# A two-block recurrent/attention kernel: one small weight product from rounded parts and residues, and the second row group's normalisation ahead of three chunks

## The reference, cut to what matters

```
xn = layernorm(x)
s  = attn(xn)                      # layer 0: recurrent cell, layer 1: attention
g  = silu(ffn(xn, W1, W2, W3))     # silu(xn W1^T) * (xn W3^T), Hadamard transform, times W2^T
x  = x + s * g
```

```
out = ((xn @ W_in^T) * k) @ W_out^T      # = xn @ M,  M = W_in^T diag(k) W_out^T, 256 x 256
s   = xn + rmsnorm(out) * norm_w
```

## Time and profile before

| what | value |
|---|---|
| time, median of 3 runs | 355.51 us (355.45 to 355.77) |
| the profiled execution | 356.1 us, of which the span of the trace is 354.3 us |
| PE busy | 348.0 us, 98% of the span |
| DVE busy | 250.6 us, 71% |
| ACT busy | 170.4 us, 48% |
| POOL busy | 108.3 us, 31% |
| granted TensorE clock | full (1.00) through the whole span |

### The profile page before, as it was taken

One profiled execution on the slowest core, in us unless ns is written; L12 is line 12 of the kernel. 1 busy time (PEld: TensorE's weight loads), 2 busy tenths in 40 slices (PEclk: granted clock), 3 DMA queues, 4 the chain that ended last, 5 costly groups with the idle time before them and its releaser, 6 DMA issues.

```text
span 354.3 us, 4946 instructions
## 1 busy us (share of the span) xinstructions
PE 348.0 (98%) x1761; PEld 295.3 (83%) x1761; DVE 250.6 (71%) x491; ACT 170.4 (48%) x336; POOL 108.3 (31%) x125
## 2 busy tenths in 40 slices
PE   7999999999999999999999999999999999999996
PEld 4877888888888888888978878888888888888896
DVE  5679964995589766967588886787657887367624
ACT  2855452447245613445365544654446444464531
POOL 2163510365226943664015030160300703004011
PEclk9999999999999999999999999999999999999999
DMA  8989759306161403140242501526014251064001
GB/s 259 221 185 225 150 105 120 100 2 159 20 159 20 120 0 118 27 125 0 89 146 49 136 0 59 170 50 194 8 42 153 74 152 57 0 192 127 9 0 61
DMA packets 69664, 34.44 MB, mean 97 GB/s; under 512 B 40708, under 2 KB 69640, under 8 KB 69640
## 3 DMA queue, kind: packets, MB, share of 16 engines
q1 hardware_dynamic: 69224, 33.80, 38.1%
q10 hardware_dynamic: 416, 0.33, 0.3%
HBM read 21.99 MB, written 12.12 MB: 96 GB/s over the span
## 4 chain that ended last, share of the span: by engine, by line
PE 90%; SPq 4%; DMA 2%; ACT 2%; DVE 2%; issue 0%; ACTq 0%
PE GU L360 19%; PE GU L361 19%; PE GU L362 19%; PE O L360 8%; PE O L362 8%; PE O L361 8%; SPq L245 1%; DMA stage<-in_L_ffn_W 1%; SPq L236 1%; PE O L428 1%; SPq L306 1%; DMA X<-in_L_attn_x 1%; PE O L510 1%; PE O L509 1%; PE O L508 1%; PE T L362 1%
## 5 line engine op out<-in xcount | busy, mean ns | idle before, releaser
L724 ACT ACTIVATE hf<-GU 128x512 f32<-128x512 f32 x64 | 38.1, 598 | 79.9 <-DVE hid L851 63.7
L1007 DVE TENSOR_TENSOR hf<-hf,GU 128x512 f32<-128x512 f32 x64 | 43.5, 679 | 28.5 <-PE GU L362 22.6
L851 DVE TENSOR_TENSOR hid<-hf,hid 128x512 fp32r<-128x512 f32 x64 | 50.6, 791 | 0.3
L360 PE MATMUL GU<-XT,W1T 128*128 128x512 f32 x128 | 50.7, 396 | 0.1
L362 PE MATMUL GU<-XT,W1T 128*128 128x512 f32 x128 | 49.9, 390 | 0.0
L361 PE MATMUL GU<-XT,W1T 128*128 128x512 f32 x128 | 49.9, 390 | 0.0
L360 PE MATMUL GU<-XT,W3T 128*128 128x512 f32 x128 | 49.9, 390 | 0.0
L362 PE MATMUL GU<-XT,W3T 128*128 128x512 f32 x128 | 49.8, 389 | 0.0
L361 PE MATMUL GU<-XT,W3T 128*128 128x512 f32 x128 | 49.8, 389 | 0.0
L360 PE MATMUL O<-hid,W2hi 128*128 128x512 f32 x112 | 43.9, 392 | 0.0
L361 PE MATMUL O<-hid,W2hi 128*128 128x512 f32 x112 | 43.7, 390 | 0.0
(11 more groups left out here) (204 smaller groups left out, 725.0 us busy)
## 6 DMA issues: line engine op xcount, KB each, us to landing
swap_rows<-GX SPq DMA_DIRECT2D x7, 512.0 KB, 3.3
sT<-swap_rows SPq DMA_DIRECT2D x28, 128.0 KB, 2.8
swap_gate<-GX SPq DMA_DIRECT2D x7, 512.0 KB, 2.9
sT<-swap_gate SPq DMA_DIRECT2D x28, 128.0 KB, 2.7
stage<-in_L_ffn_W SPq DMA_DIRECT2D x12, 256.0 KB, 4.4
swap_p<-PX SPq DMA_DIRECT2D x4, 640.0 KB, 3.3
PL<-swap_p SPq DMA_DIRECT2D x16, 160.0 KB, 3.2
stage<-in_L_ffn_W SPq DMA_DIRECT2D x32, 64.0 KB, 2.7
```

Of the source, the lines that this page charges most:

```text
L360: pe.matmul(o, lhs(0), rhs(0), start=start, stop=False)
L724: act.activation(hf[:, c % 2, :], GU[:, c % 2, 0, :], ACT.Silu).then_inc(silu_done, 1)
L851: dve.tensor_tensor(dst, src, hi_part.bitcast(F32), ALU.subtract).then_inc(done, 1)
L1007: dve.tensor_tensor(hf[:, c % 2, :], hf[:, c % 2, :], GU[:, c % 2, 1, :], ALU.mult).then_inc(mul_done, 1)
```

## The change

W_in and W_out are no longer multiplied as plain float32. ACT writes the scaled W_in rounded into a new tile `winH`, and DVE computes the residue `winL` = win * k - winH, four instructions of 256 columns. The turned W_out is rounded into `woutH` by two ACT instructions of 512 columns, and DVE subtracts for `woutL`, two more. `small_m` becomes eight `mm3`, 24 float32r matmuls of 256 columns. In SBUF `winL` and `woutL` lie over `win` and `woutT`.

The order of the head changes with it. On DVE, stats(1) with its wait for xnext_loaded goes before chunk 0, normalise(1) before chunk 1, x_turn(1) before chunk 2 and turn_wout before chunk 4. On POOL rstd_of(1) goes before the first butterflies. The new residues stand between DVE's chunks 4 and 5, the two roundings of W_out between ACT's chunks 4 and 5.

```diff
             def small_m():
-                pe.wait_ge(win_scaled, MC)
-                pe.wait_ge(wout_turned, MC // 2)
+                pe.wait_ge(win_lo, MC)
+                pe.wait_ge(wout_lo, MC // 2)
 ...
-                        last = pe.matmul(O[:, 0, k * D:(k + 1) * D], win[:, m, k * P:(k + 1) * P], woutT[:, m, :],
-                                         start=(m == 0), stop=(m == MC - 1))
+                        last = mm3(O[:, 0, k * D:(k + 1) * D], lambda a: (winH, winL)[a][:, m, k * P:(k + 1) * P],
+                                   lambda a: (woutH, woutL)[a][:, m, :], m == 0, m == MC - 1)
 ...
                 for m in range(MC):
-                    act.activation(win[:, m, :], win[:, m, :], ACT.Identity, scale=kvec[:, m:m + 1]).then_inc(win_scaled, 1)
+                    act.activation(winH[:, m, :], win[:, m, :], ACT.Identity, scale=kvec[:, m:m + 1]).then_inc(win_hi, 1)
                 chunk(0, 4, True)
+                for h in (0, 1):
+                    hi(woutH[:, 2 * h:2 * h + 2, :], woutT[:, 2 * h:2 * h + 2, :], wout_turned, h + 1, wout_hi)
                 chunk(0, 5, True)
 ...
+            def win_residue():
+                for m in range(MC):
+                    dve.wait_ge(win_hi, m + 1)
+                    dve.scalar_tensor_tensor(winL[:, m, :], win[:, m, :], kvec[:, m:m + 1], winH[:, m, :].bitcast(F32), ALU.mult, ALU.subtract).then_inc(win_lo, 1)
 ...
                 nat_lo(0, w2nat)
+                dve.wait_ge(xnext_loaded, 16)
+                stats(1, TILES)
                 chunk(0, 0)
                 pair_lo(0, 1, 1)
                 nat_lo(1, w2nat)
+                normalise(1, TILES)
                 chunk(0, 1)
                 pair_lo(0, 2, 2)
                 nat_lo(2, w2nat)
+                x_turn(1)
                 chunk(0, 2)
                 k_vector()
                 chunk(0, 3)
-                dve.wait_ge(xnext_loaded, 16)
                 pair_lo(0, 3, 3)
                 nat_lo(3, w2nat)
-                stats(1, TILES)
+                turn_wout()
                 chunk(0, 4)
-                normalise(1, TILES)
-                turn_wout()
+                win_residue()
+                for h in (0, 1):
+                    lo(woutL[:, 2 * h:2 * h + 2, :], woutT[:, 2 * h:2 * h + 2, :], woutH[:, 2 * h:2 * h + 2, :], wout_hi, h + 1, wout_lo)
                 chunk(0, 5)
-                x_turn(1)
                 chunk(0, 6)
 ...
+                rstd_of(1)
                 pair_butterfly(0, 0, 1)
                 pair_butterfly(0, 1, 2)
                 quad_butterfly(0, 0, 4)
                 pair_butterfly(0, 2, 3)
-                rstd_of(1)
                 pair_butterfly(0, 3, 4)
```

More of the change, by code:

```diff
@@ L112, in two_block_kernel @@
         with ExitStack() as early:
-            win = sb("win", [P, MC, D], F32, early)
-            woutT = sb("woutT", [P, MC, D], F32, early)
+            with ExitStack() as sooner:
+                win = sb("win", [P, MC, D], F32, sooner)
+                woutT = sb("woutT", [P, MC, D], F32, sooner)
+            winL = sb("winL", [P, MC, D], F32R, early)
+            woutL = sb("woutL", [P, MC, D], F32R, early)
+            winH = sb("winH", [P, MC, D], F32R, early)
+            woutH = sb("woutH", [P, MC, D], F32R, early)
             wo = sb("wo", [P, KC, D], F32, early)
@@ L188, in two_block_kernel @@
         wout_loaded, wqkv_loaded, wo_loaded = sem("wout_loaded"), sem("wqkv_loaded"), sem("wo_loaded")
-        wout_turned, wqkv_turned, win_scaled = sem("wout_turned"), sem("wqkv_turned"), sem("win_scaled")
+        wout_turned, wqkv_turned = sem("wout_turned"), sem("wqkv_turned")
+        win_hi, win_lo, wout_hi, wout_lo = sem("win_hi"), sem("win_lo"), sem("wout_hi"), sem("wout_lo")
         xnext_loaded = sem("xnext_loaded")
```

## The result

The changed kernel takes 356.28 us (median of 22 runs, 355.81 to 357.70) where the kernel before took 355.51 (22 runs): the ratio is 1.002, with a 95% interval of 1.0013 to 1.0028. That is 0.77 us slower, where 0.1 was forecast, and 0.13 above the upper end of the range.

The account below looks back on a forecast made before the run. PE was taken to bound the kernel (90% of the chain). Product -0.57, moved work 0, residues 0, wait for small residues +0.63 gave +0.06, taken as +0.1: 355.6 us against the median 355.51, range 354.85 to 356.15.

Parts of the forecast that it names:

- upper end of the range: Top of the forecast time, 356.15 us, described as the upper end of A and half way to C.
- The product: small_m on PE: 24 float32r matmuls instead of eight float32 ones save 0.57 us in all.
- The moved statistics: stats(1) on DVE after nat_lo(0): doesn't wait; whole move of group 1's work worth 0, bounds -0.1 and +0.1.
- The new waits of small_m: PE's waits for the new residues: ready at 33.1, wanted at 35.48, so they cost nothing.
- What is late next: Chain from POOL's butterflies to small_lo(2), before the down products: 0.3 us later, so PE starts them at about 48.05.
- Sum: Product -0.57, moved work 0, residues 0, wait +0.63: +0.06, up to 0.1 more for starting anew; +0.1 taken.
- The recorded alternative with 0.395: Chain before the down products, with 0.395 us per win_residue: 0.45 later, down products at 48.2.
- E: Rival: float32r matmuls of small_m don't gain, chain 0.3 late hidden in slack, 355.5 us; chance 0.08.
- B: Rival: small_lo(2) ends in time and the whole saving stays, -0.57, 354.95 us; chance 0.15.
- C: Rival: W_in residues on DVE take 0.6 us each, chain 1.3 later, +1.1, 356.6 us; chance 0.07.
- D: Rival: rows of x land late, DVE holds nat_lo(1) from PE; 356.6 us if landing at 13.7; chance 0.02.
- A: The forecast itself: PE waits after recurrent_mix, between -0.25 and +0.5, 355.25 to 356.0 us; chance 0.68.

Follow-up runs that it names:

- e1: Kernel before with only the changed order of DVE and POOL, old float32 product, no residues: 355.48 us against 355.43 before.
- e8: Changed kernel without DVE's six residue instructions, the matmuls taking rounded parts instead: 355.64 us against 355.63 for the kernel before.
- e3: Changed kernel with PE's wait for small_av's last residues moved behind group 0's down products: 355.15 us against 355.43 for the kernel before.
- e11: Kernel before with two more four-column ACT instructions in the head, results unread: 355.86 us against 355.50 before.
- e17: Changed kernel with six more four-column ACT instructions in the head: 355.86 us against 355.52 for the kernel before.
- e7: Changed kernel run again, unedited, beside the kernel before on one chip: 356.24 us against 355.58.
- e9: Changed kernel with the old eight float32 matmuls on rounded parts, residues computed and waited for but unused: 356.22 us against 355.63 before.
- e16: Changed kernel with PE's wait moved behind group 0's down products, one W_out rounding, v's roundings merged: 354.74 us against 355.39 for the kernel before.
- e15: Kernel before with eight more four-column ACT instructions in the head: 355.39 us against 355.39 before.
- e2: Changed product and residues, but group 1's statistics, normalise, x_turn and rstd_of in the old order: 362.34 us against 355.43 for the kernel before.
- e13: Changed kernel with PE's wait moved behind group 0's down products, one W_out rounding and residue instead of two: 355.06 us against 355.50 before.

## Why the prediction was wrong

**Right.** The product: 0.57 forecast, 0.58 found. The moved statistics: nothing (e1). The new waits of small_m: nothing; the residues of W_out ended at 33.0, PE came at 34.95. The step "What is late next" named the place where the gain goes and its mechanism. PE waits 0.63 us for small_lo(2); w2_sums gets through no sooner than POOL however early DVE comes; the residues push hid_lo(4) into POOL's pair (L1230 at 1.24 us). e8 and e3 show it by taking the residues or the wait away.

**The step that failed: "Sum".** It put the change of the span on the time, which gives nothing to the part of an execution that lies around the span. That part grew by 0.33 us. With the span alone, 0.34 longer by the distances, the time would have been 355.51 + 0.34 = 355.85, within the forecast's own 355.25 to 356.0. No row of the trace could have told the rest, as it is not in the trace. e11 shows that two more ACT instructions in the head are enough for it, and e17 that six more take it away. 0.34 + 0.33 = 0.67, against 0.66 in e7 and 0.77 in the first comparison.

**Wrong in size: "What is late next".** The chain was to be 0.3 us later. Measured from POOL's first start to the end of small_lo(2) it is 47.63 - 32.73 = 14.90 against 47.67 - 33.25 = 14.42: 0.48 later. Against POOL's first start, POOL ended 0.2 us later than forecast (7.65 us, where 40.7 - 33.25 = 7.45 was forecast), in two parts of about 0.1. One is the residues of W_in: I took 0.33 us a piece, from the row with SBUF operands, where the row of the same operation in the earlier trace rows was right: 1.67 us for four, 0.395 apart. The residues of W_out then reach into POOL's first butterfly (0.90 instead of 0.73), where the forecast had them end before it. The other is POOL's last butterfly: the working gave it 2.3 us, from the end of hid_lo(5), and it takes 2.40 with no residue in it, 0.07 behind L1237. The recorded alternative with 0.395, 0.45 later, comes near the 0.48, but has only the first part of it. The start after the wait cost 0.1, which I had as an upper bound. In the span that makes +0.34 instead of the forecast +0.1.

**The rivals.** E would have the sum end at 355.5; e9, which is its kernel, shows the opposite: the chain holds up even the old product, since its slack was 0.3 and it is 0.48 later. The others did not come: PE does wait, against B; the residues of W_in took 0.395 us a piece, not 0.5, against C; and PE has no wait at the Hadamard product, against D. The upper end of the range is also not what its sentence says: half way from the 356.0 of A to the 356.6 of C is 356.3, and 356.15 is a quarter of the way.

**Open.** Why ACT's number of instructions works outside the span, and in this manner: 1.81 at four fewer, 1.81 at three fewer (e16), 1.78 to 1.82 at none, 1.99 at one more, 2.12 at two, 1.82 and 1.81 at eight. The kernels at -3 and +1 differ in other things too; e11 and e15, at +2 and +8, do not but for the spare tile. Whether it comes before the first instruction or after the last can't be read from the trace.

## What to carry to other kernels

When PE gains, look which chain of the other engines ends last at its next wait, and follow it back to the engine that doesn't hurry because PE does; here that was GpSimd, and the remedy was to move a wait that guarded nothing before the down products. In this kernel each VectorE subtraction or sum of two SBUF operands, and each tensor_scalar of the normalisation, took turns with GpSimd's instructions where it met them; count them so, and put such work where GpSimd is idle. See also whether a new wait is long enough to bring the granted clock down: in e2 this cost 1.8 us on top of the waits. For changes below a microsecond, compare span and time of many executions: a third of a microsecond can lie outside the span and change with a few instructions of an idle engine.

## What the runs showed of the hardware

- normalise's four tensor_scalar instructions of 256 columns took 1.38 us with POOL idle (before), 1.58 with one butterfly beside them (changed) and 4.22 beside four of POOL's tensor_tensor (e2).
- DVE's sum of two SBUF operands took 1.59 us beside the last 0.5 us of a POOL instruction (before) and 2.97 beside the last 1.9 us of one (changed); both ended 1.08 us after POOL.
- After 3.44 us without a matmul PE's granted clock fell to half of full, 0.7 us after PE had started again, and stood there from 46.4 to 49.8 us (e2).
- The first matmul after a wait of PE is followed 0.34 us later by the next, not 0.23; even a wait of 0.1 us costs the other 0.1 (e8, e9).
- The mean time outside the span was 1.78 to 1.81 us for the kernel before in six jobs (single executions 1.74 to 1.95). It was 1.99 us in the kernel with one more ACT instruction (e13), 2.11 to 2.14 in those with two more, but 1.82 again at eight.
